# Writing out the attention's loops over pairs of super blocks on four engines

## The chip, the cores and the metric

The kernel runs on one core of one Trainium2 chip. The metric is the device time of one execution in microseconds (us); lower is better. Engines are named as in the profile: PE is TensorE's matmul, PEld its weight load, DVE the vector engine, ACT the scalar engine, POOL GpSimd, SP the engine that issues DMAs. A "q" behind an engine's name (DVEq) is its sequencer, the part that fetches instructions, follows branches and computes registers before the engine itself gets work.

## The reference

Four graph layers over the same 4096 nodes with 128 features, each followed by a residual sum and a layer norm. The dense 4096 x 4096 matrix `adj` is multiplied with the features in the first, third and fourth; the second is a masked attention, and it alone is touched here:

```
def _L1_gnn_ref(x, adj, beta):
    norm2 = jnp.linalg.norm(x, axis=1, keepdims=True)
    cos = beta * (x @ x.T) / (norm2 @ norm2.T + 1e-07)
    masked = cos + (1.0 - adj) * -1000000000.0
    P = jax.nn.softmax(masked, axis=1)
    return P @ x
...
x = _layernorm(x + _L0_gnn_ref(x, adj, adj, ...), axis=-1)
x = _layernorm(x + _L1_gnn_ref(x, adj, L1_gnn_beta), axis=-1)
x = _layernorm(x + _L2_gnn_ref(x, adj, ...), axis=-1)
x = _layernorm(x + _L3_gnn_ref(x, adj, ...), axis=-1)
```

## The kernel before, in words

Each engine has its own program, written by hand as one block; engines meet only at counting semaphores. fp32 products are made from parts: a matrix is split into a high part (`H`) and a low part (`L`), and three products (H·H, L·H, H·L) are summed.

Before and after the attention, `multiply` streams `adj` in tiles of 128 x 2048 through the ring `raw`: ACT makes the high part (line 432), DVE the low part (line 686), TensorE multiplies (lines 1007, 1009, 1014).

The attention works on 16 super blocks (`NSB` = 16) of two row blocks of 128 rows each. `super_block(sbi, parity, more, before)` exists on TensorE, ACT and DVE. It has 16 steps k. At each step TensorE turns four 128 x 128 pieces of the exponentials (`turn_batch`, line 1083), makes a piece of the scores of a later super block (`scores`, lines 1067 to 1069), and adds the previous step's product of probabilities and features (`sum_batch`, lines 1098 to 1100). ACT takes the exponentials (line 497), row sums of `adj` (line 490) and the high part `ptH` of the turned pieces (line 505). DVE adds the mask to the scores and takes their maximum (`mask`, line 836), makes the low part `ptL` (line 854), and for k = 1, 7, 11, 15 also `ptH` (line 850). `sum_batch` waits for DVE's `ptL` of its step, so a late DVE stops TensorE at line 1098. The output of the previous super block is copied at k = 0 (`o_copy`, ACT line 510) and scaled on DVE at k = 5 (`o_rows`, lines 861 to 868).

`mask` also holds an `If` (line 822): three vector instructions that these inputs don't need. With these inputs every `If` jumps over them.

`parity` says which half of the buffer `kept` a super block uses, so loops run over pairs of super blocks. A `Fori` loop is a loop of the engine's sequencer: at its end a compare-and-branch jumps back, and semaphore values and addresses that depend on the counter are computed in registers (rows `REGISTER_ALU` and `ISA` below). The loops over pairs:

- ACT, line 581, and DVE, line 911: super blocks 1 to 12, six rounds of two, so five jumps back and one exit.
- TensorE, line 1136: super blocks 3 to 12, five rounds.
- POOL, line 388: `sbi` 1 to 15, fifteen rounds; it prepares weights (`stage_unit`) and the mask's bias (`mask_bias`, line 376).
- SP, line 312: loads the rows of `adj` for the mask; this loop stays as it is.

Super block 0 and super blocks 13 to 15 are already written out on TensorE, ACT and DVE. In the built program the loop's body, from its first instruction to its branch, has 383 instructions on DVE, 488 on TensorE, 132 on ACT and 41 on POOL.

Of the kernel before, what the change touches and what calls it, by code (L numbers as in the profile page):

```python
# [49 lines left out]
def build(nc, x_rows, adjT, adj, early, late, norms, out):  # L50
# [12 lines left out]
    NSB = NB // 2  # L63
# [14 lines left out]
    with ExitStack() as ctx:  # L78
# [50 lines left out]
        def p(name, a=0, b=None):  # L129

            t, (at, w) = (par, early_at[name]) if name in EARLY else (lpar, late_at[name])
            return t[:, at + a:at + (w if b is None else b)]
# [103 lines left out]
        def rounds(eng, n, peel):  # L236

            yield from range(peel)
            if n > peel:
                with eng.Fori(peel, n) as it:  # L240
                    yield it

        def wait_alone(eng, semaphore, value):

            eng.wait_ge(semaphore, value)
            if not isinstance(value, int):
                eng.sem_inc(waits_passed, 1)
# [89 lines left out]
        @block.gpsimd  # L337
        def _(pool):
            def stage(pass_index, split, beside=None):

                for it in rounds(pool, BK, 1 if pass_index == 0 else 0):
                    wait_alone(pool, yL_ready, it + (split * BK + 1))
                    for r in range(BPB):
                        b = it * BPB + r
                        if not (pass_index == 0 and isinstance(it, int) and it == 0 and r < 2):

                            pool.wait_ge(tile_used, it * (2 * BPB) + (pass_index * TILES + 2 * r - 2))
                        pool.tensor_copy(wH[:, r % 2, :], yH[:, bass.ts(b, D)].bitcast(F32))  # L348
                        pool.tensor_copy(wL[:, r % 2, :], yL[:, bass.ts(b, D)].bitcast(F32)).then_inc(w_ready, 1)  # L349
                    if beside is not None:  # L350
                        beside(it)

            for q in range(4):
                stage(q, q)

            def stage_unit(rb, r, nth):

                if nth is not None:
                    pool.wait_ge(s_ready, nth)
                if not (isinstance(rb, int) and rb == 0):  # L360
                    wait_alone(pool, bw_ready, rb)
                c = bass.ts(rb, D)
                pool.tensor_tensor(tmp, unitH[:, c].bitcast(F32), unitL[:, c].bitcast(F32), ALU.add).then_inc(bw_step, 1)
                wait_alone(pool, bw_step, rb * 3 + 1)
                pool.tensor_scalar(tmp, tmp, p("beta"), 0.0, ALU.mult, ALU.add).then_inc(bw_step, 1)
                wait_alone(pool, bw_step, rb * 3 + 2)
                pool.tensor_copy(wH[:, r, :], tmp).then_inc(bw_step, 1)
                wait_alone(pool, bw_step, rb * 3 + 3)
                pool.tensor_tensor(wL[:, r, :], tmp, wH[:, r, :].bitcast(F32), ALU.subtract).then_inc(bw_ready, 1)

            def mask_bias(rb, r):

                for h in range(2):
                    wait_alone(pool, deg_done, rb * 2 + h + 1)
                    t = rowbuf[:, r, h * HALF:(h + 1) * HALF]
                    pool.tensor_scalar(t, t, -1.0, MASK, ALU.add, ALU.mult).then_inc(bias_ready, 1)  # L376


            mask_bias(0, 0)
            pool.wait_ge(umax_ready, 1)  # L380
            pool.partition_all_reduce(umax[:, 1:2], umax[:, 0:1], D, RMAX).then_inc(umax_all, 1)
            pool.wait_ge(tile_used, 4 * TILES)
            pool.wait_ge(unitL_ready, 1)
            for r in range(2):
                stage_unit(r, r, None)
            mask_bias(1, 1)
            pool.wait_ge(unitL_ready, BK)
            with pool.Fori(1, NSB) as sbi:
                for r in range(2):
                    stage_unit(sbi * 2 + r, r, sbi * (2 * NCH) + (r + 1 - 2) * NCH)  # L390
                    mask_bias(sbi * 2 + r, r)
            stage(4, 5)

            def residual(c):

                wait_alone(pool, self_ready, c + 1)
                t = xrow[:, bass.ts(c, BANK)]
                pool.tensor_tensor(t, t, xT[:, bass.ts(c, BANK)], ALU.add).then_inc(sum_ready, 1)

            stage(5, 6, beside=residual)  # L400
# [3 lines left out]
        def _(act):  # L404
# [116 lines left out]
            def super_block(sbi, parity, more, before):  # L521

                nxt = sbi + 1
                first_r0, first_r1 = 2 * NCH + 1 - LEAD, 4 * NCH + 1 - LEAD
                for k in range(NBATCH):
                    if k == 0 and before:
                        o_copy(sbi - 1)
                    if k not in HIGH_BY_DVE:
                        turned_high(sbi, k)
                    if k + NBATCH - first_r1 < NCH and before:  # L530
                        exponent(sbi * 2 + 1, 2 * parity + 1, k + NBATCH - first_r1)
                    if first_r0 <= k < first_r0 + NCH and more >= 1:
                        exponent(nxt * 2, 2 * (1 - parity), k - first_r0)
                    if k >= first_r1 and more >= 1:
                        exponent(nxt * 2 + 1, 2 * (1 - parity) + 1, k - first_r1)
                    if k in (1, 3) and more >= 1:
                        degrees(nxt * 2 + 1, 1, k // 2, nxt)
                    if k in (9, 11) and more == 2:
                        degrees((nxt + 1) * 2, 0, (k - 9) // 2, nxt + 1)
                    if more == 0 and k == 3:  # L540
                        root(1, 0, EARLY_LN)
                    if more == 0 and 0 <= k - SCALE_STEPS - 3 < HBK:
                        x_turned(1, k - SCALE_STEPS - 3)
                    if not before and 1 <= k < 3:
                        normalise_and_high(k + 1)
                    if not before and 3 <= k < 3 + HBK:
                        high_of_x(HBK + k - 3)
# [30 lines left out]
                    if r == 1 and c < 2:  # L578
                        degrees(2, 0, c, 1)
            super_block(0, 0, 2, False)  # L580
            with act.Fori(0, (NSB - 4) // 2) as it:
                super_block(it * 2 + 1, 1, 2, True)
                super_block(it * 2 + 2, 0, 2, True)
            super_block(NSB - 3, 1, 2, True)
# [72 lines left out]
        def _(dve):  # L657
# [224 lines left out]
            def super_block(sbi, parity, more, before):  # L882
                for k in range(NBATCH):
                    if not before and k in X_NORMALISED_AT:
                        normalise(X_NORMALISED_AT[k])
                    if not before and k in X_SPLIT_AT:
                        low(X_SPLIT_AT[k], chunk(xrow, X_SPLIT_AT[k]), 4)
                    m = (k + LEAD - 2) // 2
                    if k % 2 == 0 and m < 2 * NCH and more >= 1:
                        mask_chunk(sbi + 1, 1 - parity, m)  # L890
                    if k % 2 == 0 and m >= 2 * NCH and more == 2:
                        mask_chunk(sbi + 2, parity, m - 2 * NCH)
                    turned_low(sbi, k)
                    if k == 5 and before:
                        o_rows(sbi - 1)
                    if k == 9 and before:
                        o_stats(sbi - 1)
                    if more == 0 and k < SCALE_STEPS:

                        scale_step(k, 1, BK + EARLY_LN, 0, EARLY_LN)  # L900
                    if more == 0 and 0 <= k - SCALE_STEPS < BK - 1:
                        normalise(k - SCALE_STEPS)
# [5 lines left out]
                normalise(HBK + c)  # L908
            mask_chunk(1, 1, 0)
            super_block(0, 0, 2, False)  # L910
            with dve.Fori(0, (NSB - 4) // 2) as it:
                super_block(it * 2 + 1, 1, 2, True)
                super_block(it * 2 + 2, 0, 2, True)
            super_block(NSB - 3, 1, 2, True)
# [77 lines left out]
        def _(pe):  # L992
# [140 lines left out]
            super_block(0, 0, 2, False)  # L1133
            super_block(1, 1, 2, True, True)
            super_block(2, 0, 2, True)
            with pe.Fori(1, (NSB - 4) // 2) as it:
                super_block(it * 2 + 1, 1, 2, True)
                super_block(it * 2 + 2, 0, 2, True)
            super_block(NSB - 3, 1, 2, True)
# [103 lines left out]
```

## Time and profile before

| | |
|---|---|
| Runs (us) | 1777.43, 1769.85, 1774.99; median 1774.99 |
| Profiled execution, first to last instruction | 1770.8 us (no other time of this execution is given) |
| Instructions | 26215 |
| TensorE matmul busy | 1666.0 us (94%) |
| DVE, ACT, POOL busy | 81%, 70%, 23% |
| Mean granted TensorE clock | 0.975 |
| Attention, super blocks 1 to 13 | 829.8 to 1240.2 us |

TensorE is busy nearly all the time, so its idle time is what there is to win or lose; the other engines' idle time counts only where TensorE waits for them. The granted clock is a share of full speed: 1.00 is 2.4 GHz, and the trace has it at either 1.0 or 0.5 (1.2 GHz), so a mean between says for how much of a stretch it was at the lower level.

### The profile page before, as it was taken

To read this page: it belongs to the slowest core of one execution; us is meant where nothing else is said; L and a number is where in the kernel's file an instruction comes from. 1 tells how busy PE (TensorE), PEld (TensorE's weight loads), DVE (VectorE), ACT (ScalarE), POOL (GpSimd) and SP (SyncE) were. 2 spreads that over 40 slices of the span, in tenths; PEclk is the share of its full clock that TensorE was granted. 3 is DMA by queue.
4 is the path that set the end of the run, shared out by engine and by line. 5 is a ranking of instruction groups with operands and counts; after the bars stand their busy time and mean duration, and the time that the engine had idled before them with its cause. 6 is when DMAs were issued, how large, how long until landed. Compare 5 with 4: busy or idle time off the path is not lost.

```text
span 1770.8 us, 26215 instructions
## 1 busy us (share of the span) xinstructions
PE 1666.0 (94%) x8529; PEld 1391.4 (79%) x8529; DVE 1440.4 (81%) x1537; ACT 1243.5 (70%) x1220; POOL 402.4 (23%) x589
## 2 busy tenths in 40 slices
PE   7999999999998999869999999999979999799995
PEld 6888788888887888748888988899868886378884
DVE  7888888888888888888877777778788886888886
ACT  6677677677776777668777777777656776376666
POOL 1111121111111211233323333333012110023420
PEclk9999999999999999969999999999989999999998
DMA  9999699879996988733333333333368985049983
GB/s 396 387 386 383 242 349 338 336 273 343 338 338 223 345 337 338 294 143 108 136 139 139 128 118 139 143 142 142 153 257 331 344 339 205 1 171 332 332 332 113
DMA packets 60372, 444.26 MB, mean 251 GB/s; under 512 B 6368, under 2 KB 10624, under 8 KB 10752
## 3 DMA queue, kind: packets, MB, share of 16 engines
q1 hardware_dynamic: 60288, 443.36, 66.5%
q8 instruction: 25, 0.41, 0.1%
q14 instruction: 59, 0.48, 0.1%
HBM read 441.23 MB, written 2.11 MB: 250 GB/s over the span
## 4 chain that ended last, share of the span: by engine, by line
PE 81%; DVE 10%; ACT 4%; issue 3%; DMA 2%; DVEq 0%; POOL 0%; SPq 0%; ACTq 0%; POOLq 0%
PE ps L1014 18%; PE ps L1007 18%; PE ps L1009 18%; PE ps L1083 5%; PE ps L1098 3%; PE ps L1100 3%; PE ps L1099 3%; PE ps L1067 3%; PE ps L1069 3%; PE ps L1068 3%; DVE aL L686 2%; ACT aH L432 2%; DVE ptL L854 2%; DMA raw<-adjT 1%; DVE xrow L782 1%
## 5 line engine op out<-in xcount | busy, mean ns | idle before, releaser
L686 DVE TENSOR_TENSOR aL<-raw,aH 128x2048 fp32r<-128x2048 f32 x336 | 776.3, 2315 | 139.9 <-ACT aH L432 139.1
L432 ACT ACTIVATE aH<-raw 128x2048 fp32r<-128x2048 f32 x336 | 645.8, 1922 | 269.0 <-PE ps L1009 236.2
L1007 PE MATMUL ps<-aH,wH 128*128 128x512 f32 x1536 | 414.4, 392 | 13.2 <-ACT aH L432 10.4
L1014 PE MATMUL ps<-aL,wH 128*128 128x512 f32 x1536 | 413.3, 391 | 4.2 <-DVE aL L686 3.5
L1009 PE MATMUL ps<-aH,wL 128*128 128x512 f32 x1536 | 412.8, 391 | 0.0
L348 POOL CAST wH<-yH 128x128 fp32r (+1 forms) x192 | 146.3, 762 | 988.1 <-PE ps L1014 809.9
L1007 PEld LDWEIGHTS ps<-aH,wH 128*128 128x128 f32 x1536 | 289.1, 189 | 74.4 <-POOL wL L349 10.4
L1014 PEld LDWEIGHTS ps<-aL,wH 128*128 128x128 f32 x1536 | 287.8, 188 | 69.6 <-DVE aL L686 10.4
L1009 PEld LDWEIGHTS ps<-aH,wL 128*128 128x128 f32 x1536 | 289.9, 189 | 60.8
L854 DVE TENSOR_TENSOR ptL<-ps,ptH 128x512 fp32r<-128x512 f32 x256 | 176.6, 690 | 75.1 <-ACT ptH L505 72.5
L376 POOL TENSOR_SCALAR raw<-raw 128x2048 f32<-128x2048 f32 x64 | 122.6, 1916 | 306.9 <-ACT raw L490 306.7
L505 ACT ACTIVATE ptH<-ps 128x512 fp32r<-128x512 f32 x192 | 114.4, 596 | 103.3 <-PE ps L1083 98.8
L836 DVE CUSTOM_DVE_ANT_0 kept<-ps,raw 128x1024 f32<-128x1024 f32 x128 | 155.9, 1218 | 28.7 <-issue 22.3
L1098 PE MATMUL ps<-ptH,yH 128*128 128x256 f32 x512 | 150.6, 294 | 20.3 <-DVE ptL L854 18.6
L1083 PE MATMUL ps<-par,kept 128*128 128x128 f32 x1024 | 155.4, 275 | 0.0
L497 ACT ACTIVATE kept<-kept,nmax 128x1024 f32<-128x1024 f32 x128 | 145.9, 1142 | 0.7 <-DVE nmax L840 0.7
L1100 PE MATMUL ps<-ptH,yL 128*128 128x256 f32 x512 | 145.2, 284 | 0.0
L1099 PE MATMUL ps<-ptL,yH 128*128 128x256 f32 x512 | 144.4, 282 | 0.0
L1098 PEld LDWEIGHTS ps<-ptH,yH 128*128 128x128 f32 x512 | 97.5, 190 | 46.1 <-DVE ptL L854 35.5
L686 DVE TENSOR_TENSOR aL<-kept,aH 128x2048 fp32r<-128x2048 f32 x48 | 110.0, 2293 | 26.8 <-ACT aH L432 26.8
L1067 PE MATMUL ps<-aH,wH 128*128 128x512 f32 x256 | 123.3, 482 | 5.3 <-DVE cmax L836 5.2
L490 ACT ACTIVATE raw<-raw 128x2048 f32<-128x2048 f32 x64 | 122.1, 1909 | 0.5 <-DMA raw<-adj 0.4
(122 smaller groups left out, 1556.0 us busy)
## 6 DMA issues: line engine op xcount, KB each, us to landing
raw<-adjT SPq DMA_DIRECT2D x336, 1024.0 KB, 5.6
raw<-adj SPq DMA_DIRECT2D x32, 2048.0 KB, 7.8
kept<-adjT SPq DMA_DIRECT2D x16, 1024.0 KB, 7.6
xrow<-x_rows SPq DMA_DIRECT2D x2, 1024.0 KB, 7.1
xT<-norms SPq DMA_DIRECT2D x1, 2048.0 KB, 6.9
out<-xrow SPq DMA_DIRECT2D x8, 256.0 KB, 3.2
lpar<-late SPq DMA_DIRECT2D x1, 576.0 KB, 11.8
par<-early SPq DMA_DIRECT2D x1, 228.0 KB, 16.8
```

Of the source, the lines that this page charges most:

```text
L432: nc.scalar.activation(aH[:, h, :], src, ACT.Copy).then_inc(aH_ready, 1)
L686: dve.tensor_tensor(aL[:, h, :], src, aH[:, h, :].bitcast(F32), ALU.subtract).then_inc(aL_ready, 1)
L836: dve.tensor_tensor_reduce(kept[:, slot, c * CH:(c + 1) * CH], S2[c % 2], rowbuf[:, r, c * CH:(c + 1) * CH], 1.0, LOWEST, ALU.add, ALU.max ...
L854: dve.tensor_tensor(ptL[:, k % 2, :], ps[:, PT_BANKS[k % 2], :], ptH[:, k % 2, :].bitcast(F32), ALU.subtract).then_inc(ptL_ready, 1)
L1007: pe.matmul(b, wH[:, r, :], aH[:, h, c], start=first and r == 0, stop=False)
L1009: ins = pe.matmul(b, wL[:, r, :], aH[:, h, c], start=False, stop=False)
L1014: ins = pe.matmul(b, wH[:, r, :], aL[:, h, c], start=False, stop=done)
L1067: pe.matmul(o, wH[:, r, :], unitH[:, col], start=True, stop=False)
L1083: ins = pe.transpose(ps[:, PT_BANKS[k % 2], (2 * a + r) * D:(2 * a + r + 1) * D], kept[:, 2 * parity + r, j * D:(j + 1) * D], ident)
L1098: pe.matmul(o, yH[:, jc], ptH[:, k % 2, cols], start=(j == 0), stop=False)
L1099: pe.matmul(o, yH[:, jc], ptL[:, k % 2, cols], start=False, stop=False)
L1100: ins = pe.matmul(o, yL[:, jc], ptH[:, k % 2, cols], start=False, stop=(j == NB - 1))
```

## The change: loops become written-out code

The four `Fori` loops become loops of the program that builds the kernel. Each round is then emitted as its own instructions, with semaphore values and addresses as constants. What is computed, the order of the work, the waits and the DMAs stay the same.

```
             mask_bias(1, 1)
             pool.wait_ge(unitL_ready, BK)
-            with pool.Fori(1, NSB) as sbi:
+            for sbi in range(1, NSB):
                 for r in range(2):
                     stage_unit(sbi * 2 + r, r, sbi * (2 * NCH) + (r + 1 - 2) * NCH)
                     mask_bias(sbi * 2 + r, r)
...
             super_block(0, 0, 2, False)
-            with act.Fori(0, (NSB - 4) // 2) as it:
+            for it in range(0, (NSB - 4) // 2):
                 super_block(it * 2 + 1, 1, 2, True)
                 super_block(it * 2 + 2, 0, 2, True)
             super_block(NSB - 3, 1, 2, True)
...
             super_block(0, 0, 2, False)
-            with dve.Fori(0, (NSB - 4) // 2) as it:
+            for it in range(0, (NSB - 4) // 2):
                 super_block(it * 2 + 1, 1, 2, True)
                 super_block(it * 2 + 2, 0, 2, True)
             super_block(NSB - 3, 1, 2, True)
...
             super_block(0, 0, 2, False)
             super_block(1, 1, 2, True, True)
             super_block(2, 0, 2, True)
-            with pe.Fori(1, (NSB - 4) // 2) as it:
+            for it in range(1, (NSB - 4) // 2):
                 super_block(it * 2 + 1, 1, 2, True)
                 super_block(it * 2 + 2, 0, 2, True)
             super_block(NSB - 3, 1, 2, True)
```

The built program grows from 2161 to 3264 instructions on DVE, from 3159 to 4849 on TensorE, from 1308 to 1618 on ACT and from 240 to 407 on POOL. The register instructions inside the loops go: DVE and ACT have none left.

On DVE, the end of the loop's body before: the last step (k = 15) of the round's second super block, then the branch back; the row behind it belongs to super block 13 and runs only after the last round. Pure waits are not among these rows.

```order
L847 REGISTER_ALU
L849 REGISTER_ALU
L850 CAST ptH<-ps 128x512
L851 REGISTER_ALU
L854 TENSOR_TENSOR ptL<-ps,ptH 128x512
L911 REGISTER_ALU
L911 COMPARE_AND_BRANCH
L822 COMPARE_AND_BRANCH
```

The same place in the change, where super block 3 follows super block 2:

```order
L850 CAST ptH<-ps 128x512
L854 TENSOR_TENSOR ptL<-ps,ptH 128x512
L822 COMPARE_AND_BRANCH
L827 TENSOR_SCALAR kept<-xT,epsu 128x1024
L829 RECIPROCAL kept<-kept 128x1024
L831 TENSOR_TENSOR ps<-ps,kept 128x1024
L822 UNCONDITIONAL_BRANCH
L836 ISA kept,cmax<-ps,raw 128x1024
```

The register instructions and the branch back are gone, and the next super block's `If` stands right behind the last `ptL`.

On DVE, inside a super block before: from the end of `o_rows` (k = 5) to the next mask (k = 6). The rows L824 to the second L822 are what the `If` jumps over.

```order
L868 SCALAR_TENSOR_TENSOR xrow<-ps,rsum,xrow 128x128
L868 ISA
L868 SCALAR_TENSOR_TENSOR xrow<-ps,rsum,xrow 128x128
L822 COMPARE_AND_BRANCH
L824 ISA
L827 REGISTER_ALU
L827 TENSOR_SCALAR kept<-xT,epsu 128x1024
L829 RECIPROCAL kept<-kept 128x1024
L831 TENSOR_TENSOR ps<-ps,kept 128x1024
L822 UNCONDITIONAL_BRANCH
L245 ISA x2
L836 ISA kept,cmax<-ps,raw 128x1024
```

The same place in the change:

```order
L868 SCALAR_TENSOR_TENSOR xrow<-ps,rsum,xrow 128x128 x2
L822 COMPARE_AND_BRANCH
L827 TENSOR_SCALAR kept<-xT,epsu 128x1024
L829 RECIPROCAL kept<-kept 128x1024
L831 TENSOR_TENSOR ps<-ps,kept 128x1024
L822 UNCONDITIONAL_BRANCH
L836 ISA kept,cmax<-ps,raw 128x1024
```

Both L868 instructions now follow each other, and no register instruction stands ahead of the mask.

## Rows read from the trace of the kernel before

**Rows 1.** The page: span, and busy time by engine.

```profile
span 1770.8 us, 26215 instructions
PE 1666.0 (94%) x8529; PEld 1391.4 (79%) x8529; DVE 1440.4 (81%) x1537; ACT 1243.5 (70%) x1220; POOL 402.4 (23%) x589
```

**Rows 2.** Windows from one `o_copy` to the next; columns as in the first line.

```profile
core 0: us, PE busy (x) PEld busy (x) DVE busy (x) ACT busy (x) POOL busy (x), PEclk, DMA share, GB/s
829.84:860.45 30.61, 30.26 (x212) 27.48 (x211) 24.25 (x46) 23.84 (x38) 10.85 (x12) 1.00 0.38 140
...
891.01:925.26 34.25, 32.06 (x212) 28.86 (x211) 25.33 (x46) 23.93 (x38) 10.82 (x12) 0.95 0.34 124
...
955.83:990.08 34.25, 32.09 (x212) 28.90 (x211) 25.35 (x46) 23.94 (x37) 10.83 (x12) 0.95 0.34 123
...
1020.61:1053.17 32.56, 30.50 (x212) 27.46 (x211) 25.24 (x46) 23.94 (x38) 10.85 (x12) 1.00 0.36 130
...
1083.73:1116.36 32.63, 30.54 (x212) 27.49 (x211) 25.25 (x46) 23.94 (x38) 10.84 (x12) 1.00 0.36 129
...
1146.92:1179.48 32.56, 30.51 (x212) 27.48 (x211) 25.25 (x46) 23.93 (x38) 10.86 (x12) 1.00 0.35 129
1179.48:1210.01 30.53, 30.23 (x212) 27.55 (x211) 24.19 (x46) 23.84 (x38) 10.87 (x12) 1.00 0.38 138
1210.01:1240.19 30.18, 30.08 (x212) 27.54 (x211) 24.11 (x46) 23.81 (x38) 10.83 (x12) 1.00 0.38 140
```

**Rows 3.** The chain, 829.84 to 1210.01: first and last of five such pieces.

```profile
889.39 3.26 issue
...
1145.30 3.12 issue
```

**Rows 4.** The chain, 889 to 896: start us, us, what; around the first piece.

```profile
889.33 0.06 DVEq L911
...
892.65 0.04 DVEq L911
```

**Rows 5.** Timeline, 889 to 896: idle time and its releaser in brackets.

```profile
893.21 1.22 DVE L836 CUSTOM_DVE_ANT_0 kept<-ps,raw 128x1024 f32<-128x1024 f32 x1 [3.28 <-issue]
895.10 0.43 PE L1098 MATMUL ps<-ptH,yH 128*128 128x256 f32 x1 [1.88 <-DVE ptL L854]
```

**Rows 6.** Timeline of DVE at the loop's last branch, 1208.3.

```profile
1208.24 0.69 DVE L854 TENSOR_TENSOR ptL<-ps,ptH 128x512 fp32r<-128x512 f32 x1
1208.85 1.21 DVE L836 CUSTOM_DVE_ANT_0 kept<-ps,raw 128x1024 f32<-128x1024 f32 x1
```

**Rows 7.** Waits, 829.84 to 1210.01: total us, times, longest us.

```profile
DVE kept L836 <- issue: 22.3, 29, 3.3
ACT oT L510 <- PE ps L1100: 20.2, 13, 1.6
PE ps L1098 <- DVE ptL L854: 11.3, 17, 1.9
```

**Rows 8.** The page's group of line 836: its idle time over the whole execution.

```profile
L836 DVE CUSTOM_DVE_ANT_0 kept<-ps,raw 128x1024 f32<-128x1024 f32 x128 | 155.9, 1218 | 28.7 <-issue 22.3
```

**Rows 9.** Sequencer rows of three lines: ns min/median/max, first to last start us.

```profile
L911 DVEq COMPARE_BRANCH  x6: 50/56/56, 889.3 to 1208.3; - x6
L581 ACTq COMPARE_BRANCH  x6: 40/45/45, 886.9 to 1205.9; - x6
L822 DVEq COMPARE_BRANCH  x128: 56/56/67, 773.7 to 1261.1; - x128
```

**Rows 10.** Timelines of DVE: the mask behind `o_rows`, super blocks 12 and 13.

```profile
1191.19 1.22 DVE L836 CUSTOM_DVE_ANT_0 kept<-ps,raw 128x1024 f32<-128x1024 f32 x1 [0.20 <-issue]
...
1221.45 1.23 DVE L836 CUSTOM_DVE_ANT_0 kept<-ps,raw 128x1024 f32<-128x1024 f32 x1
```

**Rows 11.** DMA queues, 829.84 to 891.01: packets, MB, share of 16 engines.

```profile
q8 instruction: 4, 0.07, 0.5%
q14 instruction: 6, 0.05, 0.3%
```

More of the change, by code:

```diff
@@ L387, in _ @@
             pool.wait_ge(unitL_ready, BK)
-            with pool.Fori(1, NSB) as sbi:
+            for sbi in range(1, NSB):
                 for r in range(2):
@@ L580, in _ @@
             super_block(0, 0, 2, False)
-            with act.Fori(0, (NSB - 4) // 2) as it:
+            for it in range(0, (NSB - 4) // 2):
                 super_block(it * 2 + 1, 1, 2, True)
@@ L910, in _ @@
             super_block(0, 0, 2, False)
-            with dve.Fori(0, (NSB - 4) // 2) as it:
+            for it in range(0, (NSB - 4) // 2):
                 super_block(it * 2 + 1, 1, 2, True)
@@ L1135, in _ @@
             super_block(2, 0, 2, True)
-            with pe.Fori(1, (NSB - 4) // 2) as it:
+            for it in range(1, (NSB - 4) // 2):
                 super_block(it * 2 + 1, 1, 2, True)
```

## The prediction

> **What bounds the kernel now.** The page comes first: TensorE is busy 1666.0 of 1770.8 us [rows 1], so only its 105 us of idle time and its clock can give anything. The change touches the attention alone, so I cut that stage into windows from one output copy to the next, one super block long, all with the same 212 matmuls [rows 2]. The reader is to see three kinds of window. Seven of the twelve in which DVE and ACT loop take 30.53 to 30.61 us, with TensorE busy all but 0.3 us. Five take longer: two 34.25 us, three 32.56, 32.63 and 32.56. And the one super block that every engine but POOL and SP runs as written-out code, 1210.01 to 1240.19, takes 30.18 us, with TensorE busy 30.08 of it. The five long windows are every second one: those that begin where DVE's pair loop jumps back.
>
> The chain over the twelve looped windows says what happens there: among thousands of short pieces it has five of 3.12 to 3.26 us called "issue", time in which an engine waited for nothing that the profile shows [rows 3]. The chain around the first of them names the place [rows 4]: DVE's sequencer executes the branch of line 911 at 889.33, and its next row, again line 911, is at 892.65. In between it executed nothing. The timeline shows who pays: DVE idles 3.28 us before the mask (line 836), so its next `ptL` is late, and TensorE idles 1.88 us at line 1098 [rows 5]. DVE had some 1.4 us in hand, so TensorE loses less than DVE. The counter-example is the loop's sixth branch, at 1208.3, which is not taken: the mask starts at 1208.85, when the `ptL` before it ends [rows 6]. So it is the jump back that costs, not the place in the work.
>
> **What the change is worth.** *DVE's jumps back.* The five long windows sum to 166.25 us; five quiet ones at their mean of 30.56 us, (380.17 - 166.25) / 7, would be 152.80. That is 13.45 us. Three of the five cost 2.0 us each; the other two cost 3.69, and in these the granted clock is 0.95 [rows 2], so TensorE was at its 1.2 GHz level for 0.05 x 2 x 34.25 = 3.4 us, right after it had stood idle, which costs the other 1.7. Written out, no jump back is left, and the stall and its clock go together. The next super block's mask is then late by nothing: its scores are there, as in the sixth round.
>
> *DVE's register instructions.* A quiet looped window is 30.56 us, the written-out one 30.18. DVE shows why: behind `o_rows`, the mask starts after 0.20 us of "issue" in super block 12 and directly behind line 868 in super block 13 [rows 10]; this step's `ptL` ends later by it, and TensorE waits. Of the 29 times that line 836 waited for issue in the twelve windows [rows 7], five are the jumps; the other 24, two a super block, share 22.3 - 16 = 6 us. TensorE's waits there say the same: 11.3 us in 17 times [rows 7], five at the jumps of 1.7 to 1.9 us and twelve of 0.2. The saving is 12 x (30.56 - 30.18) = 4.6 us. It could be less, down to nothing, if super block 13 is quicker for another reason; it has the same instruction counts and DMA share, so I take all of it.
>
> *TensorE's, ACT's and POOL's loops* I cost at nothing. TensorE already runs super blocks 1 and 2 written out, and the first window (30.61) is no quicker than the last looped one (30.53). ACT's branch takes 45 ns [rows 9], and what follows is hidden: its next instruction, the output copy, waits for TensorE every time, 20.2 us in 13 times [rows 7]. POOL is busy 10.85 us of a window. If the cover on ACT were gone, a jump there could cost at most what DVE's did; it shows no sign of it.
>
> *What is added* is code: 1103 instructions on DVE, 1690 on TensorE. Sequencers must fetch it, 4 packets of 16 KB on queue 8 and 6 of 8 KB on queue 14 in two windows in which TensorE was already written out [rows 11], against a window's some 4 MB of `adj`. Below, that costs nothing: those windows are no longer than others. Above, it costs on DVE what the jump back cost, 2.0 to 3.7 us each time that an instruction isn't there when it is needed. Nearest to what the change makes is the written-out code that is there, since it is the same code: line 836's idle time on issue is 22.3 us over the whole execution [rows 8] and 22.3 us in the looped windows, so none in written-out ones. These had 32 of the 128 jumps over an `If` [rows 9] (12 x 8 = 96 are in the loop). I take nothing, and keep the upper bound for a rival.
>
> The Trainium skill bears on the first term at two places. Its page "Advanced Engine Details and Errata", section Control Flow Timing, gives some 108 ns for a compare-and-branch; five would be 0.5 us, and by it the first term would be 0.5 and not 13.45. The row agrees about the branch itself (56 ns), but the sequencer did nothing for 3.26 us after it, so the measurement decides. Its page "Runtime: NRT & Kernel Launch", section Instruction fetch mechanics, says that code is fetched ahead in order through a window of two blocks, and that a taken branch to a place outside stops until it has been fetched. By this the whole 13.45 us would go, and jumps over an `If`, which go a few instructions ahead, would cost nothing; the trace agrees on both, and also in that DVE, with 383 instructions in its body, stalls where POOL with 41 shows none.
>
> **The sum.** 13.45 + 4.56 = 18.0 us: the twelve windows become 12 x 30.18 = 362.2 instead of 380.2 us. Against the profiled execution's 1770.8 us span this gives 1752.8. What lies behind the attention moves forward as a whole. The median of the runs shown is 4.2 us above that span. If these 4.2 us lie outside the span or elsewhere, the median becomes 1775.0 - 18.0 = 1757.0. If they are the lower clock at the three jumps at which this execution escaped it (3 x 1.7 = 5), they go as well, and it becomes 1753. I can't tell these apart and take the middle, 1755.
>
> **The rivals.** *Only the jumps' stall goes.* If the 0.38 us per super block stays, the gain is 13.45: 1775.0 - 13.45 = 1761.5. For it: it rests on one window. Against it: the instruction that is later is seen, with the register instructions ahead of it. Chance 0.09.
>
> *The gap isn't the branch's.* If the branch costs only its own 56 ns and the 3.2 us belong to something that recurs every two super blocks (a fetch that the fresh code needs as well, a row's load), the first term shrinks to 5 x 0.056 = 0.3 us, and with 4.6 for the registers the time is 1770, within 0.5% of before. For it: the profile names no cause. Against it: the branch that isn't taken has no gap. Chance 0.05. The skill's 108 ns per branch would bring it out there as well.
>
> *Slower: jumps over the `If` run ahead of the fetch.* In written-out code each jump at line 822 skips instructions that must be fetched, and some land in a block that isn't there yet. DVE would then stall as at line 911, and TensorE lose 2.0 us, or 3.7 with the clock. At one such miss per super block that is 24 to 44 us against 18: 1781 to 1801. It decides from 9 misses at 2.0 us (5 at 3.7) in the 96 jumps. For it: DVE's written-out code more than doubles in the attention. Against it: 32 such jumps without one. Chance 0.06.
>
> **How the numbers follow.** The forecast, both terms gone and nothing new, has 0.78: 1749 to 1760, which is 1753 to 1757 and 3 to 4 us either way for the runs' own spread (1769.85 to 1777.43). A bigger gain has 0.02. The range goes on to the first rival, 1761.5 and the same spread: 1749 to 1765; the other two rivals, 0.11, lie outside it. A measurement of this kernel can tell about 0.5% from no change, 8.9 us, so faster means below 1766.1: 0.78 + 0.09 + 0.02 = 0.89. Within 0.5% is the second rival, 0.05; slower the third, 0.06.
>
> **What would show it.** Right: windows of about 30.2 us for super blocks 1 to 13, none above 30.6; no row of line 836 with an idle of 3 us on issue; TensorE's waits for line 854 in this stretch down from 11.3 us to under 1; the granted clock 1.00 throughout. First rival: even windows of 30.5. Second: the gap of 3.2 us still there every other window. Third: idle times of some 3 us on issue at line 836 at irregular places, and queue 14's packets just ahead of their ends. It would be wrong altogether if the stage behind the attention, or TensorE's clock there, changed by more than some us; nothing in the change touches it.

## The result, and the profile after

The changed kernel takes 1753.55 us, the median of 4 runs (1752.98 to 1755.26), against 1776.21 us (1769.85 to 1778.13) for the kernel before in the same comparison: a ratio of 0.9884, 95% interval 0.9865 to 0.9903. The profiled execution's span is 1751.8 us, 19.0 less than before; its own time is 1753.63, so 1.8 us lie around the span.

The page of the changed kernel, the rows that answer to [rows 1], [rows 8] and [rows 11]: span, busy time, the group of line 836, TensorE's first product of a batch with its idle time, and the two queues that carry instructions (packets, MB, share).

```profile
span 1751.8 us, 24580 instructions
PE 1656.9 (95%) x8529; PEld 1389.0 (79%) x8529; DVE 1439.8 (82%) x1537; ACT 1242.9 (71%) x1220; POOL 397.9 (23%) x589
...
L836 DVE CUSTOM_DVE_ANT_0 kept<-ps,raw 128x1024 f32<-128x1024 f32 x128 | 155.3, 1213 | 5.9 <-PE ps L1069 3.1
...
L1098 PE MATMUL ps<-ptH,yH 128*128 128x256 f32 x512 | 148.3, 290 | 8.6 <-DVE ptL L854 6.9
...
q8 instruction: 38, 0.62, 0.1%
q14 instruction: 46, 0.38, 0.1%
```

The mask's idle time falls from 28.7 to 5.9 us, and its first cause is no longer "issue" (22.3 us before) but TensorE's scores. Every engine does the same work as before: same counts of matmuls, vector and scalar instructions.

Windows from one output copy to the next, columns as in [rows 2]: the first three, the last of the twelve that were looped on DVE before, and super block 13.

```profile
828.92:859.02 30.10, 29.99 (x212) 27.60 (x211) 24.05 (x46) 23.82 (x38) 10.85 (x12) 1.00 0.38 142
859.02:889.21 30.19, 30.08 (x212) 27.55 (x211) 24.09 (x46) 23.83 (x38) 10.83 (x12) 1.00 0.38 140
889.21:919.29 30.08, 29.97 (x212) 27.59 (x211) 24.00 (x46) 23.81 (x38) 10.83 (x12) 1.00 0.38 141
...
1160.09:1190.20 30.11, 30.00 (x212) 27.59 (x211) 24.00 (x46) 23.83 (x38) 10.84 (x12) 1.00 0.38 140
1190.20:1220.40 30.20, 30.09 (x212) 27.56 (x211) 24.10 (x46) 23.82 (x38) 10.82 (x12) 1.00 0.38 140
```

All twelve are 30.08 to 30.19 us long and none stands out; the window that took 34.25 us at the first jump back [rows 2] takes 30.08. The twelve together are 361.28 us (828.92 to 1190.20) and were 380.17, so 18.9 of the span's 19.0 us came from here. The rest cancels: the windows begin 0.9 us earlier, and what lies behind them takes 0.8 us longer. That stretch, before and then after:

```profile
1210.01:1770.80 560.79, 511.43 (x2444) 409.08 (x2442) 455.56 (x523) 368.80 (x357) 109.41 (x150) 0.97 0.64 237
1190.20:1751.80 561.60, 511.19 (x2444) 409.43 (x2442) 457.45 (x523) 368.90 (x357) 104.14 (x150) 0.96 0.64 237
```

TensorE works as long there as before, at a granted clock of 0.96 and not 0.97. Of the change only POOL's last rounds reach into this stretch, and why its clock differs is not shown.

The timeline of DVE where super block 3 follows super block 2, the place of [rows 5]:

```profile
887.43 0.69 DVE L854 TENSOR_TENSOR ptL<-ps,ptH 128x512 fp32r<-128x512 f32 x1
888.04 1.21 DVE L836 CUSTOM_DVE_ANT_0 kept<-ps,raw 128x1024 f32<-128x1024 f32 x1
```

The mask starts as the `ptL` before it ends; the 3.28 us are gone. The waits of the twelve windows, as in [rows 7]:

```profile
DVE ptL L854 <- ACT ptH L505: 63.4, 96, 1.0
...
ACT oT L510 <- PE ps L1100: 17.7, 12, 1.5
...
PEld ps L1098 <- DVE ptL L854: 4.0, 13, 0.3
```

The row of TensorE's matmul waiting for `ptL`, 11.3 us before, is not there any more; only the weight load ahead of it still waits, 0.3 us at a time. All other engines now wait for TensorE, directly or in turn.

### The profile page after: what moved, and what is told of

The parts are those of the page before. It is cut to its first block, busy times and chain, and to the rows that moved or that the text cites. A ratio compares the mean times of both kernels' runs of the same rounds, so it can differ in the third digit from the quotient of the medians.

```text
span 1751.8 us, 24580 instructions
## 1 busy us (share of the span) xinstructions
PE 1656.9 (95%) x8529; PEld 1389.0 (79%) x8529; DVE 1439.8 (82%) x1537; ACT 1242.9 (71%) x1220; POOL 397.9 (23%) x589
## 4 chain that ended last, share of the span: by engine, by line
PE 84%; DVE 10%; ACT 3%; issue 1%; DMA 1%; POOL 0%; SPq 0%; DVEq 0%; ACTq 0%
PE ps L1014 19%; PE ps L1009 19%; PE ps L1007 19%; PE ps L1083 6%; PE ps L1098 3%; PE ps L1100 3%; PE ps L1069 3%; PE ps L1067 3%; PE ps L1099 3%; PE ps L1068 3%; DVE aL L686 2%; ACT aH L432 2%; DVE xrow L782 1%; DVE ptL L854 1%; DVE yL L690 1%
## 5 line engine op out<-in xcount | busy, mean ns | idle before, releaser
L1083 PEld LDWEIGHTS ps<-par,kept 128*128 128x128 f32 x1024 | 119.9, 141 | 2.4 <-issue 0.2
```

The source lines that it names most:

```text
L1083: ins = pe.transpose(ps[:, PT_BANKS[k % 2], (2 * a + r) * D:(2 * a + r + 1) * D], kept[:, 2 * parity + r, j * D:(j + 1) * D], ident)
```

## The experiments

The theory was: DVE's loop alone costs the time, because its body is too long to be still held when the sequencer jumps back to its start. Rivals: the other loops have a share; any jump back costs this on DVE, whatever the body's length; it is a matter of DVE and not of length; the jumps over the `If` cost something in written-out code. The times of "DVE's loop alone", "All but DVE's loop", "A shorter body" and "Four super blocks" stand beside a kernel before of 1774.20 us (1769.75 to 1779.98), those of the other four beside 1775.24 (1772.33 to 1779.65). A ratio has its 95% interval in brackets.

**DVE's loop alone.** The kernel before, with one line changed:

```
-            with dve.Fori(0, (NSB - 4) // 2) as it:
+            for it in range(0, (NSB - 4) // 2):
```

> Only DVE's pair loop is written out; TensorE, ACT and POOL keep theirs. Theory (the gain is DVE's alone: its five jumps back and its register instructions): all of it, a span of 1751 to 1754 us, windows of about 30.1 us, no idle of 3 us on issue before the mask. Rival (the other engines' loops have a share, the 0.4 us per super block above all): even windows of 30.3 to 30.5, a span of 1756 us or more.

Measured: 1757.26 us (1755.71 to 1758.17), ratio 0.9898 [0.9869, 0.9927], span 1756.3. Two of its windows, as above; the first is the one that held the first jump back:

```profile
893.62:923.79 30.17, 30.06 (x212) 27.53 (x211) 23.86 (x46) 23.95 (x38) 10.87 (x12) 1.00 0.39 140
923.79:953.87 30.08, 29.98 (x212) 27.59 (x211) 23.87 (x46) 23.85 (x38) 10.86 (x12) 1.00 0.39 141
```

The windows are those of the full change, twelve in 361.33 us (833.33 to 1194.66) against 361.28: in the attention the gain is DVE's alone, and the rival falls there. By its span alone, 1756.3, the rival would have stood; the windows decide. The expected span was missed by 2 us, and not in the windows: they begin at 833.33 and not at 828.92, after passes in which ACT waited 24.5 us for tiles of `adj` against 14.1. Behind them both kernels take the same time. That its other runs were some 3 us above the full change's as well I can't explain by anything in the twelve windows; it stays open. TensorE's loop, whose body has 488 instructions, still jumps back in this kernel, and no window is longer for it.

**All but DVE's loop.** The changed kernel with that one line put back:

```
-            for it in range(0, (NSB - 4) // 2):
+            with dve.Fori(0, (NSB - 4) // 2) as it:
```

> TensorE, ACT and POOL written out, DVE keeps its pair loop. Theory: nothing is gained, a span of 1768 to 1775 us; five windows of 32.5 to 34.3 us with a gap of 3.1 to 3.3 us behind line 911, the others 30.5. Rival (the other loops' share): quiet windows of 30.1 to 30.4 us, or gaps shorter than 3 us; 2 to 5 us gained.

Measured: 1773.67 us (1770.40 to 1776.82), ratio 0.9996 [0.9982, 1.001]. Four of the five long windows and a quiet one, and two of the five pieces of the chain that are called issue:

```profile
892.38:924.91 32.53, 30.48 (x212) 27.48 (x211) 25.26 (x46) 23.94 (x38) 10.85 (x12) 1.00 0.35 131
924.91:955.46 30.55, 30.24 (x212) 27.55 (x211) 23.14 (x44) 23.84 (x38) 10.83 (x12) 1.00 0.38 139
955.46:989.79 34.33, 32.07 (x212) 28.88 (x211) 25.34 (x46) 23.96 (x38) 10.84 (x12) 0.95 0.33 123
...
1083.45:1116.19 32.74, 30.48 (x212) 27.46 (x211) 25.26 (x46) 23.96 (x38) 10.87 (x12) 1.00 0.36 129
...
1146.74:1180.96 34.22, 32.05 (x212) 28.88 (x211) 25.35 (x46) 23.96 (x38) 10.84 (x12) 0.95 0.34 124
```

```profile
890.75 3.03 issue
953.84 3.26 issue
```

Nothing is gained: the twelve windows take 380.29 us (831.23 to 1211.52) against 380.17. The quiet windows are 30.55 us as before, so register instructions on TensorE, ACT and POOL cost nothing. The lower clock came behind the second and the fifth jump here, behind the first and second in the kernel before. TensorE's idle time at its first product behind the second and the fourth jump:

```profile
959.64 0.36 PE L1098 MATMUL ps<-ptH,yH 128*128 128x256 f32 x1 [1.95 <-DVE ptL L854]
1087.61 0.36 PE L1098 MATMUL ps<-ptH,yH 128*128 128x256 f32 x1 [1.95 <-DVE ptL L854]
```

With the same 1.95 us of idle time, the clock fell to 1.2 GHz behind the one (window 34.33, granted 0.95) and stayed at 2.4 GHz behind the other (32.74, 1.00).

**A shorter body by leaving out the `If`.** The kernel before with all its loops; the correction for small norms is left out:

```
-                with dve.If(small_norms > 0):
-                    dve.wait_ge(s_ready, n + 1)
...
-                    dve.tensor_tensor(S2[c % 2], S2[c % 2], corr, ALU.mult)
-                    dve.drain()
```

> All loops as before, but the If in the mask (the correction for small norms, which these inputs do not need) is left out, so that DVE's loop body has 206 instructions and not 383. Theory (it is the body's length that makes the jump back stop, since its first instructions are no longer held): no gap of 3 us, no window over 31 us, 13 us gained; the register instructions stay, so even windows of 30.2 to 30.6 us and a span of 1753 to 1758. Rival (every jump back on DVE costs 3.2 us): five windows of 32 to 34 us stay, a span of 1766 or more.

Measured: 1759.27 us (1757.77 to 1762.45), ratio 0.9917 [0.9886, 0.9947], span 1756.8. Two windows, the first of which holds a jump back, and the row of the branch:

```profile
891.44:921.91 30.47, 30.27 (x212) 27.56 (x211) 24.27 (x46) 23.84 (x38) 10.82 (x12) 1.00 0.38 139
921.91:952.27 30.36, 30.16 (x212) 27.54 (x211) 24.07 (x45) 23.82 (x38) 10.86 (x12) 1.00 0.37 139
...
L911 DVEq COMPARE_BRANCH  x6: 50/56/72, 889.7 to 1193.7; - x6
```

DVE jumps back as often as before, and a window with a jump is 0.1 us longer than one without, not 2.0 to 3.7. The rival, a price on every jump back, falls.

**A body between.** As the kernel before, but the second row block of each super block goes without the correction:

```
-                with dve.If(small_norms > 0):
+                if r == 0:
+                    with dve.If(small_norms > 0):
```

> All loops as before, the If in the mask only for the first row block of a super block (the second goes without the correction that these inputs do not need), so that DVE's loop body has 295 instructions, between the 206 that showed no gap and the 383 that showed one. Theory (the gap comes when the body no longer fits in what the sequencer holds): either five gaps of 3.1 to 3.3 us as with 383 or none as with 206, nothing between. Rival (the gap grows with the body's length): gaps of 1 to 2.5 us. I expect none: even windows of about 30.4 us.

Measured: 1759.90 us (1757.39 to 1760.61), ratio 0.9908 [0.9887, 0.9928], span 1757.9. The same two windows, and the row of the branch:

```profile
891.62:921.96 30.34, 30.15 (x212) 27.53 (x211) 24.61 (x46) 23.83 (x38) 10.87 (x12) 1.00 0.39 139
921.96:952.29 30.33, 30.14 (x212) 27.52 (x211) 23.92 (x45) 23.82 (x38) 10.87 (x12) 1.00 0.38 139
```

```profile
L911 DVEq COMPARE_BRANCH  x6: 50/56/56, 889.9 to 1193.4; - x6
```

Six branches again, five of them jumps back, and no gap: with 295 instructions in the body it is as with 206. The gap does not grow with the body; it is there with 383 and not with 295. The jump still lands on an `If` here (the first mask of the body belongs to the first row block), so it isn't the `If` at the loop's start that makes the gap.

Whether code was fetched can be read from the instruction queues. In the kernel before, from the first branch of line 911 to the last (889.33 to 1208.3), and in its first gap alone (889.39 to 892.65):

```profile
q14 instruction: 25, 0.20, 0.2%
...
q14 instruction: 1, 0.01, 0.6%
```

In the kernel with 295 instructions in the body, from its first branch to its last (889.9 to 1193.4), all queues:

```profile
q1 hardware_dynamic: 2878, 41.91, 37.8%
q8 instruction: 3, 0.05, 0.1%
```

No packet of code on queue 14 at all: five times the loop goes round on code that DVE holds. The loop without any `If` (206 instructions) shows none either. With 383 instructions 25 packets of 8 KB come, and in each of the five gaps one starts; so it is in the five gaps of "All but DVE's loop" and in the two of "Four super blocks" below. So the gap is a wait for code. TensorE's code comes on queue 8 (25 packets in a whole execution in every kernel that has TensorE's loop, 38 in every one that has it written out): from its loop's first branch to its last in the kernel before (954.9 to 1209) there is no packet on it, so TensorE holds a body of 488. The length from which a jump back costs is not the same on every engine. What lies between 295 and 383 on DVE, and whether it matters where in memory the body begins, was not tried.

**Four super blocks in a round.** As the kernel before, but on DVE:

```
-            with dve.Fori(0, (NSB - 4) // 2) as it:
-                super_block(it * 2 + 1, 1, 2, True)
-                super_block(it * 2 + 2, 0, 2, True)
+            with dve.Fori(0, (NSB - 4) // 4) as it:
+                super_block(it * 4 + 1, 1, 2, True)
+                super_block(it * 4 + 2, 0, 2, True)
+                super_block(it * 4 + 3, 1, 2, True)
+                super_block(it * 4 + 4, 0, 2, True)
```

> As before, but DVE loops over four super blocks, three rounds, so it jumps back twice and not five times; its body has some 760 instructions. Theory (a fixed price per jump back): two long windows of 32.5 to 34.3 us, ten of about 30.5, 3/5 of 13.45 us = 8 us gained, a span of 1761 to 1765. Rival (a price per length of code that is fetched again, which is the same here): as before, 1768 to 1775, the gaps longer or at other places.

Measured: 1768.27 us (1763.70 to 1770.48), ratio 0.9961 [0.9946, 0.9975], span 1768.2. A quiet window and the two long ones, and the mask's waits on issue in the twelve windows (total us, times, longest us):

```profile
923.31:953.88 30.57, 30.27 (x212) 27.56 (x211) 23.02 (x44) 23.84 (x38) 10.84 (x12) 1.00 0.38 139
953.88:988.19 34.31, 32.08 (x212) 28.89 (x211) 25.34 (x46) 23.93 (x38) 10.83 (x12) 0.95 0.34 122
...
1079.80:1113.99 34.19, 32.08 (x212) 28.89 (x211) 25.25 (x46) 23.92 (x38) 10.81 (x12) 0.95 0.34 123
...
DVE kept L836 <- issue: 8.3, 22, 3.2
```

Two jumps back, two long windows, with gaps no longer than before: a price per jump, the same with 383 and with some 760 instructions. The time by itself would fit the rival (1768 to 1775); the windows decide against it. The span lies 3 us above what was expected: the clock fell at both jumps, 3.7 us each, where 2.7 on the mean of five had been reckoned, the windows begin 1.8 us later, and what lies behind them takes 1.8 us longer than in the kernel before.

**The same on ACT.** The changed kernel, with ACT looping again, but over six super blocks, so that its body has 384 instructions (the expectation says 385) where it had 132:

```
-            for it in range(0, (NSB - 4) // 2):
-                super_block(it * 2 + 1, 1, 2, True)
-                super_block(it * 2 + 2, 0, 2, True)
+            with act.Fori(0, (NSB - 4) // 6) as it:
+                super_block(it * 6 + 1, 1, 2, True)
...
+                super_block(it * 6 + 6, 0, 2, True)
```

> The changed kernel, but ACT loops over six super blocks, two rounds, so its body has 385 instructions (132 in the kernel before) and it jumps back once. Theory (length, not the engine, makes a jump back stop): one gap of some 3 us in ACT's program at the jump, from super block 6 to 7, of which the wait for TensorE hides 1.5 us, so one window longer by 1 to 3 us; the register instructions on ACT cost nothing. Rival (it is a matter of DVE's sequencer alone): no long window, ACT's next register row 0.1 us behind its branch as before.

Measured: 1755.42 us (1754.19 to 1756.83), span 1753.4. The chain at ACT's one jump back, and the two windows around it with one behind:

```profile
1005.34 0.05 ACTq L581
...
1007.83 2.65 issue
1010.48 0.06 ACTq L581
```

```profile
979.16:1010.60 31.44, 31.34 (x222) 28.57 (x220) 23.92 (x46) 23.95 (x38) 10.86 (x12) 1.00 0.37 135
1010.60:1041.35 30.75, 29.20 (x204) 26.34 (x202) 23.75 (x44) 23.74 (x38) 10.85 (x12) 1.00 0.38 138
1041.35:1071.43 30.08, 29.97 (x212) 27.50 (x211) 23.87 (x46) 23.85 (x38) 10.88 (x12) 1.00 0.37 141
```

ACT's sequencer executes the branch at 1005.34 and its next row is at 1010.48. ACT itself still has two exponentials in its queue and idles only from 1007.83. One packet of code on queue 14 starts in this gap, between 1008.8 and 1009.1. The two windows are 1.35 and 0.66 us longer than 30.09. So the stall isn't DVE's alone: ACT has it too once its body is long, and with 132 instructions its jumps cost nothing ("DVE's loop alone", where ACT still has that loop). The other eleven windows, with register instructions on ACT, are 30.08 to 30.21.

**Written out, without the `If`.** The changed kernel with the same lines left out as above:

```
-                with dve.If(small_norms > 0):
...
-                    dve.drain()
```

> The changed kernel without the If in the mask (the correction for small norms is left out, which these inputs do not need), so that written-out DVE code has no jumps. Theory (the jumps over the If cost TensorE nothing where the code is written out; TensorE sets the pace): windows of 30.0 to 30.1 us, within 2 us of the changed kernel. Rival (a part of the jumps lands in code not yet fetched and DVE's slack only hides most of it): 3 us or more faster than the changed kernel, windows under 29.9.

Measured: 1755.16 us (1752.94 to 1756.31), beside 1754.20 (1752.96 to 1754.88) for the changed kernel on the same chip. Two windows:

```profile
891.99:922.11 30.12, 30.01 (x212) 27.61 (x211) 24.02 (x46) 23.82 (x38) 10.83 (x12) 1.00 0.37 140
922.11:952.21 30.10, 29.99 (x212) 27.60 (x211) 24.01 (x46) 23.82 (x38) 10.80 (x12) 1.00 0.38 141
```

No difference: jumps over the `If` are free in written-out code. TensorE is busy in all but 0.1 us of each window, so a faster DVE could give next to nothing here.

**The changed kernel again**, for comparison with the last two:

> The changed kernel again on the same chip, for comparison with the two others that start from it: windows of 30.1 us, a time of 1752 to 1758 us; its executions spread over less than those of the kernel before, whose clock falls at some of its jumps back.

Measured: 1754.20 us, ratio 0.9876 [0.9857, 0.9895]; its windows are 30.07 to 30.20 us, as the first time.

## Why the prediction was right

**What bounds it, and the jumps back (13.45 us).** Right, by its own steps. Without the jumps nothing is left of the five gaps, and nothing came in their place; DVE's loop alone, written out, brings all of it within the windows, and all the others bring nothing. The second rival (the gap belongs to something else that recurs) fell, the third (jumps ahead of the fetch) too: 96 more jumps over an `If` stand in written-out code, and the mask never waits on issue. Instruction packets on queue 14 fell from 59 to 46 in the whole execution while TensorE's on queue 8 rose from 25 to 38. The loop with 383 instructions fetched code in every round, so writing it out fetches no more; the loop with 295, which fetched none, has only 33 on queue 14. One reading was loose and carries nothing: the branch's own row, 56 ns [rows 9], is half of the 108 ns with which the prediction has it agree.

**The second term (4.56 us).** The mechanism held in the main, since DVE was late by what its sequencer does between instructions, and the size was a little low: 12 x (30.56 - 30.11) = 5.4 us. The window of super block 13 that served as a model, 30.18 us, is itself 0.1 us longer than its neighbours now. And the name that I gave it, register instructions, covers only a part: looped windows without the gap are 30.35 us with half of the `If`s (364.17 us in twelve) and 30.11 written out, so 0.24 us per super block goes with the loop as such. The other 0.2 goes when half of the `If`s leave the looped body. It is not a price of each `If`: without any ("A shorter body") the twelve windows have a mean of 30.42, no less. It is the one behind `o_rows`, whose mask belongs to the second row block. The mask there with half of the `If`s, and TensorE's weight load that waits for this step's `ptL`, in the kernel before, with half of the `If`s, and written out:

```profile
933.46 1.22 DVE L836 CUSTOM_DVE_ANT_0 kept<-ps,raw 128x1024 f32<-128x1024 f32 x1
...
938.87 0.19 PEld L1098 LDWEIGHTS ps<-ptH,yH 128*128 128x128 f32 x1 [0.54 <-DVE ptL L854]
...
935.35 0.19 PEld L1098 LDWEIGHTS ps<-ptH,yH 128*128 128x128 f32 x1 [0.34 <-DVE ptL L854]
...
932.50 0.19 PEld L1098 LDWEIGHTS ps<-ptH,yH 128*128 128x128 f32 x1
```

The mask's 0.20 us on issue [rows 10] are gone with this `If`, although the register instructions stay, and gone without them, although the `If` stays: here only the two together made DVE's sequencer late. The prediction misread one of its rows. TensorE's twelve waits of 0.2 us [rows 7] are not behind `o_rows` but at the end of each super block, behind the last step's `ptL`:

```profile
1208.99 0.39 PE L1098 MATMUL ps<-ptH,yH 128*128 128x256 f32 x1 [0.20 <-DVE ptL L854]
```

They stay in both loops with fewer `If`s and go when the loop is written out, so they belong to the 0.24.

**What was costed at nothing.** TensorE's, ACT's and POOL's loops: shown to be nothing by the second experiment. The bound that I kept for ACT (a jump there could cost at most what DVE's did, if its cover were gone) held: with a body too long, ACT's jump costs 2.0 us of windows.

**From span to median.** Here the middle of two readings was taken, 1755, and 1753.55 came. The sum on the span gave 1752.8 and the span is 1751.8. What lies around the span is 1.8 us, so the rest of the distance to the median was variation between executions. Over 26 runs of the kernel before, the time goes with the mean granted clock: 1769.75 us at 0.982, 1779.60 at 0.971, a correlation of -0.88. In the three profiles whose DVE jumps back with a stall, the clock fell at 2 of 5, 2 of 5 and 2 of 2 jumps, 1.7 us each; in the seven profiles without such a stall on DVE it never fell in these windows. The second reading's number, 1753, is the nearer one, and, as it implies, the medians differ by more (22.7 us) than the spans of the two profiles (19.0). But that the clock at the jumps makes this difference is not shown: both profiles with five jumps lost it at two, and the clock is low at times outside the attention as well (0.97 and 0.96 behind the windows). That 1755 came within 1.5 us is in part luck; the two readings lay only 4 us apart.

## What to carry to other kernels

A loop of a sequencer costs next to nothing while its body is short, and a few microseconds per round once the sequencer no longer holds the body's start. Look for a piece of the chain called issue between a branch and the next sequencer row, for a packet of code on the instruction queue within it, and compare it with the last round, whose branch is not taken. Either shorten the body or write the loop out, and only on the engine that shows the gap: here one line on DVE gave all that four loops gave in the windows, and TensorE's longer body never stalled. Price it by what the bounding engine loses (2.0 us), not by the gap (3.2 us), and add the clock where that engine then runs at its lower level.

## What the runs showed that was not expected

- The step is sharp: DVE's jump back cost TensorE about 0.1 us with 206 and nothing measurable with 295 instructions in the body, and 2.0 to 3.7 us with 383 and some 760. TensorE's jump back, with 488, cost nothing.
- ACT's sequencer stood still for 5.1 us at its jump (1005.39 to 1010.48), longer than DVE's 3.0 to 3.3. On both the packet of code starts about 1 us behind the end of the last instruction that the engine still had (ACT: 1007.83, packet between 1008.8 and 1009.1; DVE at the first jump of the kernel before: 889.93, packet between 890.8 and 891.2). That the sequencer waits for its engine before it asks for code would explain the difference; it is not shown.
- TensorE's clock fell to 1.2 GHz for 3.4 us at some jumps and not at others. In the three profiles it fell behind six of the seven idle times of 1.80 to 1.95 us, and behind none of the five of 1.74 to 1.77; of two of 1.95 us in the same execution it fell behind one.
- Straight code asked for fewer instruction packets on queue 14 than the loop that stalled (46 against 59), and for more than the loop that fitted (33).
